# The wide program's TensorE operands moved to the front of their memory, 128 bytes beyond a multiple of 512

## What is computed

```
gate = x Wg' + 0.5 (x Ag[i]') Bg[i]'        up = x Wu' + 0.5 (x Au[i]') Bu[i]'
act  = silu(gate) * up                       1376 features
down = act Wd' + 0.5 (act Ad[i]') Bd[i]'     512 features
m    = max(|down|) over the features of a token, at least 1e-5
out  = x + ((down / m) Q') * m * scale + bias
```

## Time and profile before

| | before |
|---|---|
| median of 3 runs | 927.63 us (926.81 to 929.03) |
| profiled execution | 929.12 us, span 927.1 us |
| mean granted TensorE clock | 0.994 |
| TensorE matmuls, busy | 3930, 893.9 us (96%) |
| weight loads, busy | 3930, 715.5 us (77%) |
| VectorE, ScalarE, GpSimd busy | 347.4, 260.4, 81.1 us |
| DMA | 45.38 MB, mean 49 GB/s |

### The profile page before, as it was taken

The page is one execution under the profiler, slowest core; times in us unless marked ns, Lnnn a source line. Parts: engine busy times, 40 slices in busy tenths (PEclk is TensorE's granted clock), DMA queues, the critical chain, the costliest instruction groups (busy, mean ns, idle before and its releaser), DMA issues.

```text
span 927.1 us, 13664 instructions
## 1 busy us (share of the span) xinstructions
PE 893.9 (96%) x3930; PEld 715.5 (77%) x3930; DVE 347.4 (37%) x754; ACT 260.4 (28%) x448; POOL 81.1 (9%) x110
## 2 busy tenths in 40 slices
PE   2999999999999999999999999999999999999994
PEld 2778778887877887888788787888878878878873
DVE  3563345222532234422452324432254223542223
ACT  2442243111522124211242213411152222422112
POOL 0011003010030000300003100121003000201100
PEclk9999999999999999999999999999999999999998
DMA  3556121111112011020111101111111111210001
GB/s 97 145 161 176 36 59 34 44 34 30 44 40 55 23 35 51 27 66 11 50 48 35 46 13 54 54 38 34 32 45 45 49 29 32 58 32 25 12 15 48
DMA packets 45445, 45.38 MB, mean 49 GB/s; under 512 B 13168, under 2 KB 31984, under 8 KB 45392
## 3 DMA queue, kind: packets, MB, share of 16 engines
q1 hardware_dynamic: 43024, 41.85, 16.8%
q10 hardware_dynamic: 2368, 3.02, 1.2%
HBM read 36.44 MB, written 8.39 MB: 48 GB/s over the span
## 4 chain that ended last, share of the span: by engine, by line
PE 92%; SPq 2%; DMA 2%; DVE 2%; ACT 1%; issue 1%; DVEq 0%; ACTq 0%
PE pw_up L1704 25%; PE pw_down L1748 23%; PE pw_gate L1704 23%; PE ps_misc L1773 6%; PE pw_td L1737 4%; PE pw_down L1758 2%; PE pw_up L1714 2%; PE ps_misc L1704 2%; PE pw_gate L1714 2%; PE ps_misc L1765 1%; DMA wb_raw<-b_rows 1%; SPq L569 0%; DMA rows<-w_down 0%; DMA plan_room<-places 0%; SPq L306 0%
## 5 line engine op out<-in xcount | busy, mean ns | idle before, releaser
L1748 PE MATMUL pw_down<-wd,wact_split 128*128 128x512 f32 x960 | 236.3, 394 | 0.0
L1704 PE MATMUL pw_up<-wxs,wgu 128*128 128x512 f32 x948 | 228.5, 390 | 0.0
L1748 PEld LDWEIGHTS pw_down<-wd,wact_split 128*128 128x128 f32 x960 | 180.2, 188 | 47.2
L1704 PE MATMUL pw_gate<-wxs,wgu 128*128 128x512 f32 x864 | 213.0, 395 | 1.4 <-ACT wact_full L993 1.3
L1704 PEld LDWEIGHTS pw_up<-wxs,wgu 128*128 128x128 f32 x948 | 178.3, 188 | 37.7
L1704 PEld LDWEIGHTS pw_gate<-wxs,wgu 128*128 128x128 f32 x864 | 159.9, 188 | 37.0 <-issue 2.2
L1354 DVE TENSOR_TENSOR wact_full<-pw_up,wact_full 128x512 f32<-128x512 f32 (+1 forms) x87 | 60.1, 690 | 300.9 <-PE pw_up L1714 298.5
L993 ACT ACTIVATE wact_full<-pw_gate 128x512 f32<-128x512 f32 (+1 forms) x80 | 47.8, 598 | 280.6 <-PE pw_gate L1714 280.6
L1005 ACT ACTIVATE wact_split<-wact_full 128x512 fp32r<-128x512 f32 x80 | 50.6, 632 | 70.0 <-DVE wact_full L1354 70.0
L1359 DVE TENSOR_TENSOR wact_split<-wact_full,wact_split 128x512 fp32r<-128x512 f32 x80 | 55.6, 695 | 26.3 <-ACT wact_split L1005 26.2
L1773 PE MATMUL ps_misc<-wq,wdt_split 128*128 128x512 f32 x224 | 56.8, 395 | 0.0
(11 more groups left out here) (119 smaller groups left out, 665.5 us busy)
## 6 DMA issues: line engine op xcount, KB each, us to landing
out<-rows SPq DMA_DIRECT2D x120, 64.0 KB, 1.6
rows<-x_tok SPq DMA_DIRECT2D x112, 64.0 KB, 1.8
rows<-w_gu SPq DMA_DIRECT2D x8, 512.0 KB, 4.2
x_raw<-x_feat SPq DMA_DIRECT2D x60, 64.0 KB, 1.7
x_more<-x_feat SPq DMA_DIRECT2D x60, 64.0 KB, 1.8
wb_raw<-b_rows SPq DMA_DIRECT2D x32, 92.0 KB, 2.8
low_room<-b_rows SPq DMA_DIRECT2D x32, 80.0 KB, 2.5
rows<-w_down SPq DMA_DIRECT2D x9, 256.0 KB, 4.1
```

The lines of the kernel that those rows point to most:

```text
L1704: last = nc.tensor.matmul(bank, w, wxs[:, xp, k, :], start=(n == 0 and k == 0), stop=False, skip_group_check=(f == 0))
L1748: last = nc.tensor.matmul(pw_down[:, s, :], wact(ap, f)[:, s * P:(s + 1) * P], wd[:, wp, f, :], start=(f == 1 and n == 0), stop=False)
```

## The change

The calls of sb() for the wide program are put in another order. The tensors that TensorE reads, wxs, wb_split, wt_split, wact_first, wact_split, wdt_split, identity and wad_split, come directly behind wa_raw; those that it does not read (wb_raw, low_room, td_room, x_more, wad_raw, wact_full) come behind them. Names, sizes, types and the total are the same, and no line of any engine's program is another. PSUM is untouched.

```diff
             wa_raw = sb("wa_raw", [P, 2, AGU], stack=wide)
 
-            wb_raw = sb("wb_raw", [P, 2 * STARTS[FIRST]], stack=wide)
-
-            low_room = sb("low_room", [P, 3, WIDE], stack=wide)
-            td_room = sb("td_room", [P, WIDE], stack=wide)
-            x_more = sb("x_more", [P, ENTRIES, KC * SEQ], stack=wide)
             wxs = sb("wxs", [P, 2, KC, WIDE], F32R, stack=wide)
             wb_split = sb("wb_split", [P, 2, 2, P], F32R, stack=wide)
-            wad_raw = sb("wad_raw", [P, 2, FC * RANK], stack=wide)
-            wad_split = sb("wad_split", [P, 2, STACK], F32R, stack=wide)
             wt_split = sb("wt_split", [P, 2, WIDE], F32R, stack=wide)
-            wact_full = sb("wact_full", [P, 2, WIDE], stack=wide)
 
             wact_first = sb("wact_first", [P, 2, WIDE], F32R, stack=wide)
             wact_split = sb("wact_split", [P, 2, 2, WIDE], F32R, stack=wide)
             wdt_split = sb("wdt_split", [P, 2, KC, P], F32R, stack=wide)
             identity = sb("identity", [P, P], stack=wide)
+            wad_split = sb("wad_split", [P, 2, STACK], F32R, stack=wide)
+
+            wb_raw = sb("wb_raw", [P, 2 * STARTS[FIRST]], stack=wide)
+
+            low_room = sb("low_room", [P, 3, WIDE], stack=wide)
+            td_room = sb("td_room", [P, WIDE], stack=wide)
+            x_more = sb("x_more", [P, ENTRIES, KC * SEQ], stack=wide)
+            wad_raw = sb("wad_raw", [P, 2, FC * RANK], stack=wide)
+            wact_full = sb("wact_full", [P, 2, WIDE], stack=wide)
```

More of the change, by code:

```diff
@@ L153, in build @@
             wa_raw = sb("wa_raw", [P, 2, AGU], stack=wide)
+            wxs = sb("wxs", [P, 2, KC, WIDE], F32R, stack=wide)
+            wb_split = sb("wb_split", [P, 2, 2, P], F32R, stack=wide)
+            wt_split = sb("wt_split", [P, 2, WIDE], F32R, stack=wide)
+            wact_first = sb("wact_first", [P, 2, WIDE], F32R, stack=wide)
+            wact_split = sb("wact_split", [P, 2, 2, WIDE], F32R, stack=wide)
+            wdt_split = sb("wdt_split", [P, 2, KC, P], F32R, stack=wide)
+            identity = sb("identity", [P, P], stack=wide)
+            wad_split = sb("wad_split", [P, 2, STACK], F32R, stack=wide)
             wb_raw = sb("wb_raw", [P, 2 * STARTS[FIRST]], stack=wide)
@@ L159, in build @@
             x_more = sb("x_more", [P, ENTRIES, KC * SEQ], stack=wide)
-            wxs = sb("wxs", [P, 2, KC, WIDE], F32R, stack=wide)
-            wb_split = sb("wb_split", [P, 2, 2, P], F32R, stack=wide)
             wad_raw = sb("wad_raw", [P, 2, FC * RANK], stack=wide)
-            wad_split = sb("wad_split", [P, 2, STACK], F32R, stack=wide)
-            wt_split = sb("wt_split", [P, 2, WIDE], F32R, stack=wide)
             wact_full = sb("wact_full", [P, 2, WIDE], stack=wide)
[L168 to L171, removed]
             pw_down = ps("pw_down", [P, WSUBS, 512], stack=wide)
```

## The result

| | before | after |
|---|---|---|
| median | 927.37 us (6 runs, 926.81 to 929.03) | 922.74 us (6 runs, 921.59 to 923.19) |
| profiled execution, its span | 929.12, 927.1 us | 923.06, 921.1 us |
| time from tile 1's first matmul to the last matmul | 792.70 us | 787.33 us |

The ratio is 0.9944 with an interval of 0.9934 to 0.9955: 4.6 us faster, where 9.1 were forecast. The profiled execution of the kernel before was the longest of its runs, so the spans differ by more (6.0 us) than the medians. Waits in tile 0 come out differently from execution to execution; from tile 1 on, where they play no part, the difference is 5.4 us.

What follows compares the result with a forecast made beforehand. TensorE, 96% busy, was taken as the bound: number of matmuls times the distance between their starts. Savings of 11.2 us less 0.5 and 1.6 given back made 9.1, so 927.63 became 918.5 us, range 912 to 929.

Steps and rivals of the forecast that it cites:

- the signs of being right: Down projection and L1773 means 389 to 391 ns, L1748 groups 2.72 to 2.76 us, busy time falling with the span.
- The stream's distance depends on where the operands lie: 512-column matmuls on TensorE: start distance 226.7 or 233.3 ns by operand addresses modulo 512 bytes; equal remainders taken as fast.
- the two readings left open: Slow 512-column stream: it goes with the stationary operand at 0, or with a difference of 128 between the operands.
- L1773, 1.4 us: 28 groups of eight matmuls with wdt_split: from 1.86 to 1.81 us each, 1.4 us saved.
- Gate behind a slow stream, 1.1 us: 28 gate groups behind a slow stream: 2.76 to 2.72 us each, since entering from another rhythm costs about 0.04.
- L1748, 6.2 us less 1.6 at the entry: 80 groups of twelve: to 2.72 us, 6.2 saved; half of them lose 0.04 entering from L1737, 1.6 given back.
- the rival "half": L1748 never settles when entered from L1737 and keeps its 6.2 us; 4.5 us gained, 923.1 us, chance 0.15.
- Up groups and L1714, 0.8 + 0.5 us, and L1737, 0.6 us: 80 up groups 2.73 to 2.72 us, some 160 L1714 matmuls 0.23 to 0.227, 88 L1737 pairs 0.46 to 0.453.
- The wait before L1758, 0.5 us: L1758 waits for wact_first, whose copies get no shorter while the matmuls ahead do: 0.5 us given back.
- Collision of equal remainders: Rival: equal remainders slow L1704's 2112 matmuls to the slow rate, 13.9 us lost, 941.5 us, chance 0.15.

Runs made afterwards that it cites:

- e1: Changed kernel with 384 bytes of room ahead of wxs, wide operands at remainder 0, weights at 128: 934.4 us, ratio 1.0073.
- e4: Changed kernel with 64 bytes of room ahead of wxs, wide operands at remainder 192, weights at 128: 932.58 us, ratio 1.0046.
- f4: Changed kernel with zeros padding L1738's weights to 128 columns and L1715 to 128 rows: 917.09 us, ratio 0.9883.
- g1: f4 with moving minus stationary operand at +32 bytes in every pair but two: 936.56 us, ratio 1.0103.
- g3: Kernel before, its allocation order kept, with only f4's edits of shape (128 columns, 128 rows): 924.14 us, ratio 0.9967.
- f1: Changed kernel with room around wt_split, so that it alone stands at remainder 0 as before: 919.8 us, ratio 0.9911.
- the second comparison: The changed kernel measured again without an edit, against the kernel before: 922.11 us, ratio 0.9945.
- g2: As g1, with moving minus stationary operand at -32 bytes, against f4: 936.66 us, ratio 1.0097.
- e2: Changed kernel with plan ahead of wgu and 384 bytes ahead of wxs, every operand at remainder 0: 921.59 us, ratio 0.9933.
- e3: Changed kernel with 256 bytes of room ahead of wxs, wide operands at remainder 384, weights at 128: 921.29 us, ratio 0.9932.
- f3: Changed kernel with L1715 over 128 rows in place of 96, the added rows zero: 918.34 us, ratio 0.9895.

## Why the prediction was half right

The median, 922.74 us, lies in the range of 912 to 929 but just above the 914 to 922 that went with the forecast, and half of the 9.1 us came. All the signs of being right came true: L1748's mean is 391 and L1773's 389, the down group 2.76, the gate group behind L1773 2.72, the busy time falls with the span, and the wait before L1758 is 0.33 us.

- **The stream's distance depends on where the operands lie.** Right, and shown by e1 to e4. Of the two readings left open (stationary at 0, or the difference), the runs chose the difference, modulo 256 bytes. By the Trainium skill, "TensorE: Matmul & The Clock Gate", section "Step-by-step: what each phase is for", loading the next weights takes no read bandwidth from the running matmul. That addresses therefore decide nothing does not hold here: f4 and g1 differ in addresses alone, and are 917.09 and 936.56 us. Whether it is read bandwidth that is lost, no run shows.
- **L1773, 1.4 us.** Right: 1.5, mean 389, groups at 1.81.
- **Gate behind a slow stream, 1.1 us.** The number came: those 28 groups went from 2.76 to 2.72. The rest of the 1.9 is in groups that the forecast had not counted. The reason given, entry from a slow rhythm, is not enough: in g3 L1773 is as slow as before and the group behind it takes 2.72 us. So this term was right in part by luck.
- **L1748, 6.2 us less 1.6 at the entry.** The stream settles at 226.7 as forecast, so the rival "half", by which it never would, is wrong, though its 923.1 us is the number closest to the result. Its excess was 5.7 us and not 6.2. The entry was a little too small: half of the groups pay 0.04 as taken, those of the even chunks, but the others pay 0.01, in all 2.0 us for 1.6. 3.8 us were saved and not 4.6.
- **Up groups and L1714, 0.8 + 0.5 us, and L1737, 0.6 us.** This is the step that failed, and it has the wrong sign: 1.2 us were lost. I took the low-rank matmuls for small members of the same stream, for which the same rule would hold. They have another shape, and for a 96-row pair equal remainders are worse than 128 apart (f1): the up group behind it takes 2.74 us for 2.73, as three of its steps are slow and not one. Net of the wait, 9.1 us were forecast and 5.9 to 6.0 came. Of the 3.2 us that are missing this step makes 1.3 + 0.6 + 1.2 = 3.1. L1748 and L1758 add 1.1, which the gate groups, L1773 and the smaller wait make good.
- **The wait before L1758, 0.5 us.** Right in kind and half the size. The weight load's wait grew in tile 2 from 0.29 to 0.33 us, and the distance into L1758 from 0.26 to 0.29; over the eight tiles that is 0.25 us. The stream ahead gained only 0.04 us per tile, not 0.07, and 0.03 of it were given back.
- **Collision of equal remainders.** Wrong for the matmuls that it spoke of: equal is the fast case for full shape, and the difference is the slow one.
- The rest of the gap, to the 4.6 us of the medians, is that the profiled execution of the kernel before was its longest; the second comparison gave 5.3.

**Left open.** Why a difference costs 3 to 7 ns, why 64 bytes cost the up projection less than the down projection, and why the entry takes up to eight steps, no run shows. Differences of 32, 64 and 128 bytes were tried, no others. f1 gained in L1738 and the down groups too, though it moved wt_split alone; why was not tried. The gate groups behind the transposes (2.84 us) hold half of the excess that is left in f4; another place for the transposes wasn't tried.

## What to carry to other kernels

Where TensorE streams without a wait, with a weight load for each matmul as here, put all operands that it reads at one remainder of 256 bytes, streamed and loaded alike, and the permanent weights with them; pad a lone odd-shaped matmul to 128 rows and 128 columns with zeros. If it can't be padded, try it 128 bytes apart (f1). Before costing such a change, list every pair (streamed, loaded) with its shape, and treat each shape as a case of its own: a rule read from the 128-row stream had the wrong sign for the 96-row one. In the profile such a cost shows in no wait and no idle time, only in the mean length of a matmul (389 against 395 ns) and in the distances between starts.

## What the runs showed of the hardware that was not expected

- Two 512-column float32r streams of full clock and equal shape run at 226.7 or at 229.9 to 233.3 ns per matmul, by the difference of their two operands' addresses modulo 256 bytes. 0 is fast. The slow means of the up and down projections are 232.7 to 233.3 at 32 either way (g1, g2), 229.9 at +64 and 232.9 at -64 (e4), and 231.7 to 232.6 at 128 (kernel before, e1, g3). The remainder itself (0, 128, 384) plays no part (e2, e3).
- In the changed kernel a matmul of 96 rows costs the up group behind it 20 ns, in three steps; the down group behind the pair with 32- and 64-column weights loses 10 ns (odd chunks) or 35 ns (even chunks), in up to eight steps, and still 4 or 22 ns in f3, where that pair is the only odd shape before it. Padded to 128 by 128 with zeros the disturbance is all but gone (down group 2.76 to 2.72 us in f4), although more is loaded.
- A slow stream does not by itself disturb the fast one behind it: 2.72 us for the gate group behind the slow L1773 in g3.
